# Plain transposes for scaled ones, and a second graph product and a norm taken row block by row block

## The reference

```python
xn = _layernorm(x, axis=-1)
x = x + _L1_gnn_ref(xn, edge_index, ..., W_up) + _L1_mix_ref(xn[None], ..., Wo, bo, proj)[0]
x = x + _L1_ffn_ref(_layernorm(x, axis=-1)[None], gate_w, ...)[0]
# end of _L1_mix_ref
return out @ Wo + bo
```

## Time and profile before

| | us |
|---|---|
| median of 3 runs | 1893.53 |
| lowest and highest run | 1887.46, 1898.96 |
| the profiled execution's own time | 1897.03 |
| its span on the core | 1895.2 |
| TensorE busy | 1792.2 (95%) |
| VectorE busy | 744.7 (39%) |
| ScalarE busy | 390.4 (21%) |
| GpSimd busy | 644.6 (34%) |

### The profile page before, as it was taken

How to read it: one execution, slowest core, us unless ns; L and a number is a source line. 1 busy time by engine, 2 the same in 40 slices (tenths; PEclk the granted TensorE clock), 3 DMA queues, 4 the chain that set the end, 5 groups by cost and what they waited for, 6 DMA issues and landing times. The chain is left out here.

```text
span 1895.2 us, 22157 instructions
## 1 busy us (share of the span) xinstructions
PE 1792.2 (95%) x8594; PEld 1140.2 (60%) x8594; DVE 744.7 (39%) x1523; ACT 390.4 (21%) x715; POOL 644.6 (34%) x538
## 2 busy tenths in 40 slices
PE   7999999998999999999999999999999999999953
PEld 5466445544554777546677765677654676676731
DVE  5967101332524322454455557340530223222226
ACT  0000000001401011001576745211000312222222
POOL 0566881030000076777887620000300222222210
PEclk9999999999999999999899999999999999999986
DMA  9645115073530144333222145150321799999952
GB/s 344 182 113 144 2 2 155 22 223 66 214 129 5 32 123 133 92 96 86 54 54 53 37 101 154 45 223 24 102 94 45 253 415 407 401 411 410 404 161 88
DMA packets 104070, 289.09 MB, mean 153 GB/s; under 512 B 61942, under 2 KB 65240, under 8 KB 91837
## 3 DMA queue, kind: packets, MB, share of 16 engines
q1 hardware_dynamic: 28634, 224.83, 32.1%
q0 software_dynamic: 68160, 51.85, 12.3%
q10 hardware_dynamic: 7198, 11.36, 1.9%
HBM read 257.19 MB, written 30.32 MB: 152 GB/s over the span
## 5 line engine op out<-in xcount | busy, mean ns | idle before, releaser
L325 PE MATMUL bank<-wring,turned_a 128*125 128x512 f32 x480 | 207.6, 593 | 1.6 <-DVE turned_a L640 0.7
L523 POOL DMA_INDIRECT table_d<-wring x85 | 174.5, 2053 | 97.8 <-issue 63.3
L886 POOL DMA_INDIRECT wring<-xl_d,wring x85 | 109.1, 1284 | 256.4 <-DMA xr_d<-flat_b 230.5
L325 PEld LDWEIGHTS bank<-wring,turned_a 128*125 128x125 f32 x480 | 89.6, 188 | 115.3 <-issue 114.2
L2154 PEld LDWEIGHTS bank<-picked_t,wring 128*128 128x128 f32 x1280 | 145.3, 194 | 7.6 <-issue 7.3
L2154 PE MATMUL bank<-picked_t,wring 128*128 128x128 f32 x1280 | 147.2, 278 | 0.1
L341 PE MATMUL bank<-flat_d,wring 128*128 128x312 f32 (+1 forms) x512 | 135.0, 426 | 0.0
L899 POOL DMA_INDIRECT score_d<-wring x85 | 110.8, 1303 | 69.7 <-DMA score_d<-wring 47.0
L886 POOL DMA_INDIRECT wring<-xr_d,wring x85 | 111.9, 1317 | 25.9 <-issue 25.9
L341 PEld LDWEIGHTS bank<-flat_d,wring 128*128 128x128 f32 x512 | 96.7, 189 | 37.9
L2169 PE MATMUL bank<-wring,unit_t 128*128 128x512 f32 x160 | 74.0, 605 | 0.0
(11 more groups left out here) (433 smaller groups left out, 2764.8 us busy)
## 6 DMA issues: line engine op xcount, KB each, us to landing
wring<-in_experts SPq DMA_DIRECT2D x60, 2048.0 KB, 13.1
wring<-in_L_Ws SPq DMA_DIRECT2D x6, 2048.0 KB, 19.3
table_d<-eq_buf SPq DMA_DIRECT2D x2, 3072.0 KB, 30.1
score_d<-no_edge SPq DMA_DIRECT2D x2, 3072.0 KB, 33.3
wring<-table_d POOLq DMA_DIRECT2D x10, 610.4 KB, 7.3
wring<-score_d SPq DMA_DIRECT2D x5, 1093.8 KB
wring<-pid_d ACTq DMA_DIRECT2D x17, 312.5 KB
wring<-in_edge_w ACTq DMA_DIRECT2D x17, 312.5 KB
```

The costliest lines, as they stand in the source:

```text
L325: ins = pe.matmul(bank[0:R, :], act_t[:, k, tok(t)], w[:, k * HALF:(k + 1) * HALF], start=(k == 0), stop=(k == chunks - 1))
L523: pool.indirect_dma_start(out=tables_d[b % 2], out_offset=bass.IndirectOffsetOnAxis(ap=edge_at[:, b:b + 1], axis=0), in_=edge_sums[:, b, : ...
L886: pool.indirect_dma_start(out=to[:, g % 2, j, :], out_offset=None, in_=table, in_offset=bass.IndirectOffsetOnAxis(ap=index[:, b:b + 1], ax ...
```

## The change

Three things are changed.

1. The scaling of the probabilities moves. ScalarE multiplies each head's 125 by 625 block by the reciprocal sums in place (`scale_probs`, four instructions for each row block), and `turn_probs` becomes 20 plain transposes. VectorE makes no diagonal matrices any more. The first turn stands behind tile 3 and no longer behind tile 2.
2. The product with `W_up` is taken row block by row block (`up_product(t)`, four matmuls of 512 columns), behind the tiles 6 to 9, and the last one behind those. VectorE adds it, takes the statistics (`add_up`) and, at the end of the block, norms the row blocks 0 to 3. The add and the norm of row block 4 come in the next block.
3. In the next block TensorE transposes row block by row block as the norms are there; the 26 matmuls that nobody reads are gone, and so are the waits for all copies in front of the logits, each of whose five parts now waits for its own row block.

The buffer of the normed rows now lies over the buffer `turned_a`, which is made larger for it (`region_a`). The constant buffer `no_edge` shrinks from 512 to 384 columns, and the two transfers that fill the score table repeat it 16 times instead of 12. `gat_t` lies over `sq`.

```diff
-        TURN_AT = {2: 0, 4: 1, 6: 2, 7: 3, 8: 4}
+        TURN_AT = {3: 0, 4: 1, 6: 2, 7: 3, 8: 4}
         ROWS_AT = {4: 0, 6: 1, 7: 2, 8: 3, 9: 4}
+        UP_AT = {6: 0, 7: 1, 8: 2, 9: 3}
+
+        def add_up(v, t):
+            after(v, dve_step)
+            for h in range(2):
+                cols = slice(h * HALF, (h + 1) * HALF)
+                v.tensor_tensor(res[:, t, cols], dring.consume(v)[0:R, :], res[:, t, cols], ALU.add).then_inc(d_emptied, 1)
+                v.wait_ge(d_emptied, dring.taken)
+                dve_half_stats(v, res, t, h)
+            ln_tile[t] = dve_tile_var(v, t, 1e-5)
...
                 def turn_probs(t):
-                    pe.wait_ge(diags_made, t + 1)
+                    pe.wait_ge(probs_scaled, t + 1)
                     for a in range(T):
                         bank = sring.produce(pe)
                         for h in range(GH):
-                            ins = pe.matmul(bank[0:R, tok(h)], probs[:, t % 2, h, tok(a)], scale_diag[t % 2][:, h, :],
-                                            start=True, stop=True)
+                            ins = pe.transpose(bank[0:R, tok(h)], probs[:, t % 2, h, tok(a)], ident[0:R, 0:R])
...
+                def up_product(t):
+                    if t == 0:
+                        up.append(wt.take(pe))
+                    pe.wait_ge(s_emptied, gat_marks["rows", t])
+                    for h in range(2):
+                        bank = dring.produce(pe)
+                        for k in range(2):
+                            ins = pe.matmul(bank[0:R, :], gat_t[:, k, tok(t)],
+                                            up[0][:, k * D + h * HALF:k * D + (h + 1) * HALF],
+                                            start=(k == 0), stop=(k == 1))
+                        ins.then_inc(d_filled, 1)
...
                 pe_gemm_rows(pe, k1_t, beside=attend)
-                sring.wait_empty(pe)
-                pe_gemm_slot(pe, gat_t, 2)
+                up_product(T - 1)
+                wt.free(dring.filled, dring.made)
...
-                    soft.mark(v.reciprocal(gden[:, t, :], gden[:, t, :]))
-                    after(v, soft)
-                    if t >= 2:
-                        v.wait_ge(s_filled, gat_marks["turned", t - 2])
-                    v.tensor_tensor(scale_diag[t % 2], ident[0:R, 0:R].unsqueeze(1).to_broadcast([R, GH, R]),
-                                    gden[:, t, :].unsqueeze(2).to_broadcast([R, GH, R]), ALU.mult).then_inc(diags_made, 1)
+                    v.reciprocal(gden[:, t, :], gden[:, t, :]).then_inc(dens_made, 1)
...
+                    if n in UP_AT:
+                        add_up(v, UP_AT[n])
-                after(v, dve_step)
-                dve_add_to_res(v)
+                for t in range(T - 1):
+                    dve_tile_norm(v, res, shared, t, ln_tile[t])
...
+                def scale_probs(t):
+                    s.wait_ge(dens_made, t + 1)
+                    for h in range(GH):
+                        ins = s.activation(probs[:, t % 2, h, :], probs[:, t % 2, h, :], ACT.Copy, scale=gden[:, t, h:h + 1])
+                    ins.then_inc(probs_scaled, 1)
+
                 exps(0)
                 exps(1)
+                scale_probs(0)
                 for t in range(T):
                     keep_turned(t)
                     if t:
                         keep_rows(t - 1)
                     if t + 2 < T:
                         exps(t + 2)
+                    if t + 1 < T:
+                        scale_probs(t + 1)
+                    if t >= 3:
+                        act_tile_root(s, t - 3)
...
-                pe_keep_busy(pe, 26)
-                pe.wait_ge(normed.sem, normed.n + T)
-                pe_transposes(pe, shared)
-                pe_wait_evacuated(pe)
+                turned = [pe_turn(pe, shared, t, normed.n - (T - 1) + t + 1) for t in range(T)]
                 pe.wait_ge(ffn_in, 64)
-                pe_logits(pe, x3_t, gate16, NE1)
+                pe_logits(pe, x3_t, gate16, NE1, before=lambda t: pe_wait_turned(pe, turned[t]))
...
-                dve_layer_norm(v, res, shared, 1e-5, halves_done=True)
-                evac_transposes(v, dring, 0, x3_t, lambda o, i, k: v.tensor_copy(o, i))
+                add_up(v, T - 1)
+                keep_turned_rows(v, dring, 0, x3_t, 0, copy)
+                dve_tile_norm(v, res, shared, T - 1, ln_tile[T - 1])
+                for t in range(1, T):
+                    keep_turned_rows(v, dring, 0, x3_t, t, copy)
```

More of the change, by code:

```diff
@@ L370, in cols_tiles @@
                     yield m, slice(at, at + n), ring.consume(eng)[:, 0:n]
+        region_a = sb("region_a", [P, T * D])
+        turned_a = region_a[:, 0:K * N].rearrange("p (k n) -> p k n", n=N)
         mid = scope()
-        turned_a = sb("turned_a", [P, K, N], scope=mid)
         WIDE = 104
@@ L394, in gps_kernel @@
         b1_col = sb("b1_col", [P, 1], scope=l0)
-        no_edge = sb("no_edge", [P, HALF], scope=l0)
+        EDGE_C = 384
+        no_edge = sb("no_edge", [P, EDGE_C], scope=l0)
         zeros = eq_buf[:, 0:HALF]
@@ L740, in gps_kernel, with pe_logits @@
         gu_marks = {}
-        def pe_logits(pe, act_t, gate, ne):
+        def pe_logits(pe, act_t, gate, ne, before=None):
             bank = dring.produce(pe)
             for t in range(T):
+                if before:
+                    before(t)
                 for k in range(K):
@@ L961, in gps_kernel @@
         probs_t = v1_flat[:, 0:2 * T * GH * R].rearrange("r (s a h d) -> r s a h d", s=2, a=T, h=GH)
-        scale_diag = [flat[:, 0:GH * R].rearrange("r (h d) -> r h d", h=GH) for flat in (kf_flat, qf_flat)]
-        gat_t = q1_t[:, 6:8, :]
+        gat_t = sq
+        shared = region_a[0:R, :].rearrange("r (t d) -> r t d", d=D)
         DN = float(DH) ** -0.25
@@ L990, in gps_kernel @@
         WEIGH_AT = {0: 0, 1: 1, 3: 2, 5: 3, 7: 4}
-        tops_made, exps_made, diags_made = sem("tops_made"), sem("exps_made"), sem("diags_made")
+        UP_AT = {6: 0, 7: 1, 8: 2, 9: 3}
[7 more added lines that the diff above has]
+            ln_tile[t] = dve_tile_var(v, t, 1e-5)
+        tops_made, exps_made, dens_made = sem("tops_made"), sem("exps_made"), sem("dens_made")
+        probs_scaled, ln_tile = sem("probs_scaled"), {}
         soft = Steps(sem("soft"))
@@ L1235, in gat_rows @@
                     ins.then_inc(s_filled, 1)
+                    gat_marks["rows", t] = sring.made
+                up = []
+                def up_product(t):
[9 more added lines that the diff above has]
+                        ins.then_inc(d_filled, 1)
                 def attend(n):
@@ L1673, in _ @@
                         exps(t + 2)
+                    if t + 1 < T:
+                        scale_probs(t + 1)
+                    if t >= 3:
+                        act_tile_root(s, t - 3)
                 keep_rows(T - 1)
+                act_tile_root(s, 2)
+                act_tile_root(s, 3)
             @block.sync
@@ L1683, in _ @@
                 for part in range(2):
-                    sp.dma_start(score_d.rearrange("(q p n c) h -> q p n (c h)", q=2, p=P, c=HALF // GH)[part],
-                                 no_edge[:].unsqueeze(1).to_broadcast([P, 12, HALF])).then_inc(scores_clear, 16)
+                    sp.dma_start(score_d.rearrange("(q p n c) h -> q p n (c h)", q=2, p=P, c=EDGE_C // GH)[part],
+                                 no_edge[:].unsqueeze(1).to_broadcast([P, 1536 * GH // EDGE_C, EDGE_C])).then_inc(scores_clear, 16)
                 wt.issue(sp, until=GNN_LOAD + 4)
@@ L1726, in _ @@
                     load_scores(t)
-                    sp.wait_ge(diags_made, t - 1)
+                    sp.wait_ge(dens_made, t - 1)
                     load_counts(t)
@@ L1733, in gps_kernel @@
         ffn = scope()
-        shared = sb("shared", [R, T, D], scope=ffn)
         w_pick = sb("w_pick", [R, 2, T], scope=ffn)
@@ L1861, in per_row, with copy @@
                     return x.unsqueeze(2).to_broadcast([R, T, NE1])
-                dve_layer_norm(v, res, shared, 1e-5, halves_done=True)
-                evac_transposes(v, dring, 0, x3_t, lambda o, i, k: v.tensor_copy(o, i))
+                def copy(o, i):
+                    return v.tensor_copy(o, i)
+                add_up(v, T - 1)
[3 more added lines that the diff above has]
+                    keep_turned_rows(v, dring, 0, x3_t, t, copy)
                 v.wait_ge(ffn_consts.sem, 7)
@@ L1976, in _, with copy @@
             def _(s):
-                act_ln_root(s)
-                evac_transposes(s, sring, 1, x3_t, lambda o, i, k: s.activation(o, i, ACT.Copy))
+                def copy(o, i):
+                    return s.activation(o, i, ACT.Copy)
+                keep_turned_rows(s, sring, 1, x3_t, 0, copy)
+                act_tile_root(s, T - 1)
+                for t in range(1, T):
+                    keep_turned_rows(s, sring, 1, x3_t, t, copy)
                 act_router(s, r1, 2)
```

2 lines of the change are left out of this document (added).

## The result

| | before | after |
|---|---|---|
| median, us | 1895.37 | 1884.81 |
| lowest, highest of 12 runs | 1887.46, 1940.54 | 1881.87, 1888.75 |
| the profiled execution's own time | 1897.03 | 1887.77 |
| its span | 1895.2 | 1886.0 |
| from the first tile of the output GEMM to the shared expert's first GEMM | 145.5 | 141.2 |

The changed kernel takes 0.9948 of the time before, with a 95% interval of 0.9934 to 0.9961: 9.9 us less, between 7.4 and 12.5. (The 1940.54 is a disturbed run; the ratio leaves such runs out.) The forecast was 1886.1, or 7.4 us less.

What follows compares the result with a forecast made beforehand. TensorE, busy 1792.2 of 1895.2 us, was taken to bound the kernel, the logits' end moving its end one for one. Terms -11.6 - 2.8 + 4.6 + 2.4 = -7.4 us took 1893.53 to 1886.1; range 1880 to 1893.5.

Steps and rivals of the forecast that it cites:

- The turns: Output GEMM stage: 100 turn matmuls of 22.8 us become transposes of 11.2 us, -11.6 us on TensorE's path.
- wait of 0.7 for ScalarE's drain: At four turns, ScalarE emptying five banks could show at worst 0.7 us each; 0 to 2.8, taken as 0.
- The scaling: 20 new ScalarE instructions of 125x625, priced like a square at 0.724 us each, 2.9 us per row block.
- the wait of +4.6: Second turn: TensorE waits for scaling queued behind the exponentials of row block 2, ready 1159.5 against 1155.0; +4.6 us.
- the turns don't shrink: Rival: ScalarE's draining or late scaling gives back 3 to 7 us at the turns; 1889 to 1894, chance 0.16.
- ScalarE is late every time: Rival: dear scaling and ScalarE's order cost 7.1 us at each of four turns; +16.4 us, 1909.9, chance 0.05.
- the forecast of 9.8: End of the last `W_up` matmul: 1231.7 instead of 1241.5, 9.8 us earlier.
- The small load: Before the logits: `bs_b` lands at 1245.0, TensorE ready at 1240.4, so only 9.8 of 14.3 us gain remain.
- The clock at the logits: With the unread matmuls gone, the logits start at half clock: 0 to 3.2 us, taken as +2.4.
- the row of 444.1: Earlier trace window cited in the forecast: the clock rose at 444.1 after 13 records of nothing but transposes.
- The term for the first turn: First turn, moved behind tile 3: TensorE's wait of 2.33 us for VectorE's diagonal matrix goes.
- 631.6 us to the end of the kernel: Sign of being wrong: the time between the logits and the kernel's end differing from the 631.6 us of before.

Runs made afterwards that it cites:

- after_again: The changed kernel itself, run once more beside two variants on one chip: 1885.22 us, 0.9953 of the kernel before.
- gate_alone: The changed kernel with the logits waiting for the load of `gate16` alone, the other three small loads waited for behind them: 0.9925 of the kernel before.
- best_again: The changed kernel with logits waiting for `gate16` alone and scaling of t+1 ahead of exponentials of t+2, second run: 1872.95 us, 0.9893 of before.
- turn_later: The kernel before with one number changed, the first turn behind tile 3 instead of tile 2: 0.998 of the kernel before.
- gate_and_order: The changed kernel with logits waiting for `gate16` alone and scaling of t+1 ahead of exponentials of t+2, first run: 1877.04 us, 0.9902 of before.

## Why the prediction came out right, and where it was off

**The turns.** Foretold 11.2 us for 100 transposes, 11.6 less. At full clock 20 take 2.35 us as a row and 2.2 to 2.3 to the next, as foretold; 13.9 in all with the low stretch. No wait of 0.7 for ScalarE's drain showed, whose five copies take 2.50 us, not 2.95.

**The scaling.** Taken at 0.724 each by the nearest row. ScalarE's timeline, four at a time:

```profile
1139.44 2.94 ACT L1701 ACTIVATE flat_d<-flat_d,wring 125x625 f32<-125x625 f32 x4
...
1148.67 5.32 ACT L1681 ACTIVATE flat_d<-wring 125x625 f32<-125x625 f32 x4 [2.61 <-DVE wring L1495]
1153.88 2.93 ACT L1701 ACTIVATE flat_d<-flat_d,wring 125x625 f32<-125x625 f32 x4
```

0.73 each. The same three rows are the chain at the second turn, foretold in times from the start of the GEMM: tops 33.1, exponentials done 38.5, scaling done 41.5, TensorE there at 37.0. Measured: 33.3, 38.6, 41.4 and 36.8. So the wait of +4.6 (the steps as written, 1159.5 - 1155.0, make 4.5) was 4.74, put down to the scaling, and there was none at the later turns. At the fourth turn the scaling was ready 0.7 us before TensorE came, as foretold, at the third 5.3 and not 3.5. The rivals in which the turns don't shrink, or ScalarE is late every time, fall.

**What the working missed at the second turn** is the clock. The wait that it foretold had the price of a wait, but the 20 transposes and the product behind it then ran low: 4.56 - 2.35 and 2.75 - 2.35, 2.6 us more. For the logits the same mechanism was priced; here it wasn't looked for. So the last product with `W_up` ended at 1232.27, 116.9 us after the start of the GEMM, against 123.5 before: 6.6 us earlier, not 9.8. In `after_again`, with the smaller wait, it was 10.2. That the forecast of 9.8 lies so near is luck there: a wait that was too long by 2.6 us stood in for the low clock that was missing.

**The small load.** The logits were put where `bs_b` lands, 13.3 us after the last product with `W_up`; it was 12.6. TensorE was ready 4.31 us earlier (foretold 4.6), and `gate_alone` shows that this time is really to be had: its logits start 8.3 us after the last product with `W_up`. The transposes taken row block by row block are thus covered by the load, as foretold. The window of the wait shows 112 GB/s, and the earlier trace rows 130.

**The clock at the logits.** Foretold to start low for +2.4 of 0 to 3.2; measured 11.87 - 8.95 = 2.9. The direction held; but the working took the transposes and the idle time around them together. The runs part them. `gate_alone` has the same transposes with no wait behind them, and the clock is kept; with the wait filled by work it is kept too. It is the idle time of 4.3 us that did it. Transposes alone were no safety either: in `best_again` the clock fell in them, behind the wait of 2.60 us, and rose again in them. The price was small there, 0.3 us to the start of the logits against `gate_alone`, as the wait of 1.04 us that `gate_alone` has in front of its last transposes fell away. Windows of TensorE, with only transposes between 1221.0 and 1227.0:

```profile
1218.50:1221.00 2.50, 0.00 (x0) 1.00 0.60 164
1221.00:1222.30 1.30, 1.25 (x12) 1.00 1.04 441
1222.30:1225.70 3.40, 3.40 (x20) 0.52 0.93 370
1225.70:1227.00 1.30, 1.30 (x13) 0.94 0.39 133
1227.00:1235.70 8.70, 8.70 (x82) 1.00 0.33 122
```

The Trainium skill (TensorE: Matmul & The Clock Gate, "Part 4: PE-mode transpose") says that a transpose doesn't count as busy in the same way for the clock. By that rule the clock could not have risen at about 1225.7, ahead of the first matmul of the logits; here the measurement speaks against it, as the row of 444.1 had done.

**The sum.** Foretold -7.4; the changed stage had -4.3 in one profile and 137.6 - 145.5 = -7.9 in the other, and the times say -9.9 (-7.4 to -12.5), with the forecast at the interval's edge. The prediction gave most of its chance to a change within 0.5%, 9.5 us; the measured 0.52% lies on the other side of that line by less than its uncertainty. The last step from the stage to the median is the weakest. The term for the first turn was sized from one execution at 2.33 us; `turn_later` has 3.8 in the times, which fits other executions that add the low clock. And the term for the second turn, 4.6, stands on the profile before, whose scores came 2.1 us ahead of the GEMM; four of the five profiles behind it have a wait of 2.0. Against these stand the low clock at the second turn and the 0.5 us by which it was dearer at the logits. The errors thus cancel in part. With these terms the sum becomes -11.6 - 3.8 - 0.5 + 2.0 + 1.7 + 2.9 = -9.3, an estimate made after the fact from rows and from one ratio; how often each case comes isn't known, so it is no proof. The forecast of 1886.1 was also reached from a median of three runs, 1893.53, which twelve runs put at 1895.37.

**Behind the logits** I took 631.6 us to the end of the kernel, and it was 1886.0 - 1256.6 = 629.4. The matmuls are the same. In the thirteen profiles this time goes from 628.5 (`turn_later`) to 633.2 us (`gate_and_order`), and in these two the clock was at 0.50 for 46.9 and 58.0 us of it; in the changed kernel it was 51.3, in the kernel before 58.2. So the low stretches that come and go between executions go with it. By the letter of the prediction the 2.2 us would be a sign of being wrong; they are within what one kernel and the next show here, and the sign was badly chosen.

## What to carry to other kernels

When a change creates a wait in front of TensorE, count it twice: as the wait, and as the slow work behind it. Here 15 of 24 waits of 2 to 5 us were followed by 3.4 or 6.8 us at half clock, mostly for 1.6 to 3.2 us more, and all seven waits over 3 us were.

A semaphore that collects several loads makes the first consumer wait for the last of them. Before something is moved forward, ask which load it really reads: splitting this one off gave some 4 us, and the early norm alone gave nothing.

One profiled execution shows one arrival time of a slow side chain (here GpSimd's writes). Where a wait depends on such a chain, compare two profiles of the same program before its row becomes a term of a sum.

## What the hardware showed unexpectedly

- Within one program, the first load of the scores starts 2.0 us ahead of the GEMM in one execution and 5.95 in another, and in another kernel 1.0 us behind it; the Performer stage takes 203 to 205 or 208 to 210 us with the same matmuls. Neither goes with the other: `after_again` has 204.1 with the early load, the changed kernel 204.1 with the late one. What sets either wasn't found.
- A wait of 2.5 us at full clock (1218.5 to 1221.0 above) was followed by a fall 1.3 us later, in the midst of work; waits of 2.6 and 1.0 us in `gate_alone` were followed by none. In front of the turns, 1.99 us in `after_again` brought 3.4 us at 0.50, and 2.33 us in the kernel before brought none. So a wait of this size may or may not cost the clock, and a saving that rests on it is not the same in every execution.
